# Both norms' roots in one GpSimd pair, row normalisation on GpSimd, routing weights on VectorE

## The chip, the core and the metric

The kernel runs on one core of a Trainium2 chip. A core has five engines that run their own instruction lists side by side and wait for one another through semaphores: TensorE (PE in the profile; its loads of weights are PEld), VectorE (DVE), ScalarE (ACT), GpSimd (POOL), and SyncE (SP), which here only issues transfers. GpSimd also issues the transfers that scatter rows by a list of indices. The metric is the time of one execution on the device, in microseconds; less is better.

## What is computed

One layer of cross-attention and one mixture-of-experts layer over 64 x 64 = 4096 tokens of 256 numbers each:

```
q = rms(linear(layernorm(x)))          k = rms(linear(ctx))        v = linear(ctx)
x = x + linear(softmax(q k' / 4) v)    # 16 heads of 16, 64 keys for each of 64 batches
h = layernorm(x)
two experts of 8 for each token by the largest logits of h, weights from their softmax
x = x + sum over the two: weight * W2 (silu(Wg h) * (Wu h))    # inner width 176
```

Both layernorms are (x - mean) / sqrt(variance + 1e-5), without scale and shift. For two experts with logits a >= b the weights are 1 / (1 + e) and e / (1 + e), with e = exp(b - a).

## The kernel before, in words

The tokens stand in 32 tiles of 128. A first stage, attention and routing, is a software pipeline over these tiles, written out in full: in turn i each engine works on several tiles at several depths. `Tile(j, s)` is tile n = 4j + s, `slot` its place in rings of four (s mod 4), `par` in pairs of buffers; `tile(3)` in turn i is tile i - 3, `tile(-2)` is tile i + 2. Each engine's `turn` function fixes the order of its work, and no scheduler changes it. Turns 0 to 34 have work for all engines, GpSimd's go on to turn 38. A second stage runs the experts: rows of tokens sorted by expert come back from memory in 71 slots of 128 rows, go through TensorE, and are scattered to their results by GpSimd (`send_y`); TensorE sets the pace of that stage, and the change touches nothing in it.

In a turn i of the first stage, as far as the change goes:

- TensorE transposes k of tile i - 1 (`tr_k`, the first work of its turn), then x of tile i, finds the largest scores of tile i - 2, weighs the values of tile i - 3, transposes q of tile i - 1 (`tr_q`), projects k, v and q of tile i, in even turns counts rows per expert for a pair of tiles (`count_rows`), scores tile i - 2, and last projects the attention of tile i - 3 (`project_out`).
- VectorE takes remainders of ScalarE's casts (`k_lo`, `xt_lo`, `q_lo`, `att_lo`: numbers go to TensorE as a high and a low part), the maxima, `normalise`, the statistics of the first norm of tile i + 2 (`ln1_stats`, `ln1_mean`), `ln2_norm` (the second norm applied to tile i - 4: a row of 256, subtract the mean, multiply by the root), then `att_lo`, then in odd turns `choose` (the two best experts of a pair of tiles), in even turns `route` (their places among the sorted rows), then `gate_of_x`, `k_scale`, `q_scale` with the roots from `qk_rms`, and last `residual` (x plus attention, the logits, the statistics and `ln2_mean` of tile i - 3). In turns 21 to 24 and 29 it also writes parts of the plan for the expert stage.
- GpSimd has `ctx_lo` (a remainder), `send(t, 1)` and `send(t, 0)` (the scatter of a tile's rows to its second and first expert, L545), `qk_rms` (the roots that scale q and k of tile i: two columns), `ln1` (root and shift of the first norm of tile i + 2), `weights` in even turns (the pair's two expert weights), `set_ids`, `ln2` (root of the second norm of tile i - 3), and `weights_lo` (a remainder of the expert weights). A root is two instructions: multiply and add (L499), then raise to the power -0.5 (L501).
- ScalarE applies the first norm to tile i + 1 (`ln1_norm`), casts, squares, takes exponentials, copies a normalised row (`row_copy`) and takes e for the pair (`gap_exp`).
- SyncE loads x in five parts, the last two in its turns 3 and 5 (L404), and spreads q and v over SBUF; the later parts of x are waited for once each, at tiles 2, 8 and 9, by `ln1_stats`.

The waits are `need` or `wait_ge` on counts of tiles done, and a waiting instruction holds all that stands behind it on its engine.

Of the kernel before, what the change touches and what calls it, by code (L numbers as in the profile page):

```python
# [93 lines left out]
def build_in(nc, stack, x, ctx_t, w_proj, w_out, w_exp, w_gate, bias, norm_q, norm_k, out,  # L94
# [378 lines left out]
    def _(pool):  # L473
# [44 lines left out]
        def ln2(t):  # L518
            need_alone(pool, pool_passed, S["row_ready"], t.n - 1)
            inv_sqrt(t, rstd2[:, t.slot, :], veps2[:, t.par, :], mean_var2[:, t.par, 1:2], 1.0, 1e-5,  # L520
                     S["ln2_mean"], S["ln2_veps"], S["ln2_rstd"])

        def weights(a, b, pp):

            need_alone(pool, pool_passed, R["e_gap_ready"], (a.pair + 1) * 2)
            need_alone(pool, pool_passed, S["row2_ready"], b.n + 1)
            w = row[:, :, a.slot:a.slot + 2, D + 1:D + 2].rearrange("p k m d -> p k (m d)")
            pool.tensor_scalar(one_e[:, :], e_gap[:, pp, :], 1.0, 1.0, ALU.mult, ALU.add).then_inc(R["weight_set1"], 1)
            need_alone(pool, pool_passed, R["weight_set1"], a.pair + 1)
            pool.tensor_tensor(w[:, 0, :], one_e[:, :], one_neg[:, :], ALU.pow).then_inc(R["weight_set2"], 1)  # L530
            need_alone(pool, pool_passed, R["weight_set2"], a.pair + 1)
            pool.tensor_tensor(w[:, 1, :], e_gap[:, pp, :], w[:, 0, :], ALU.mult).then_inc(R["weight_set3"], 1)
# [1205 lines left out]
```

## Time and profile before

| | us |
|---|---|
| three runs | 491.95, 491.39, 489.05 (median 491.39) |
| span of the profiled execution, first to last instruction | 489.1 |
| TensorE busy | 438.3 |
| VectorE busy | 391.4 |
| GpSimd busy | 308.6 |
| ScalarE busy | 276.7 |

The page gives no time of the profiled execution besides its span. The first stage lasts to about 309 us, the expert stage to about 475, and the rest adds up results. A busy share is an average over a whole stretch; what sets the pace is read from the order in time, from what an engine was waiting for when it stood still, and from the distance between the same instruction in one turn and in the next.

### The profile page before, as it was taken

The page shows a single profiled execution, that of the slowest core. Times are in us where ns is not written, and L with a number is a line of the kernel's source. Part 1 is how long each engine was busy: PE and PEld are TensorE (multiplying, and loading weights), DVE is VectorE, ACT ScalarE, POOL GpSimd, SP SyncE. Part 2 cuts the span into 40 slices and gives each one's busy share as a digit, 9 for nine tenths or more (in the row PEclk, how much of TensorE's full clock was granted, in tenths as well). Part 3 has the DMA queues.
Part 4 walks back from the last instruction along what each step waited for, and adds up shares of the span by engine and source line. Part 5 has one row for each costly group of instructions (what it writes and reads, how often), then busy time and mean ns, then how long its engine had stood idle before and what let it go on. Part 6 is the DMA issues. An engine that isn't in the chain of part 4 may idle for free.

```text
span 489.1 us, 15233 instructions
## 1 busy us (share of the span) xinstructions
PE 438.3 (90%) x4428; PEld 381.4 (78%) x4428; DVE 391.4 (80%) x1327; ACT 276.7 (57%) x802; POOL 308.6 (63%) x529
## 2 busy tenths in 40 slices
PE   7898999999999999898999888798999999999960
PEld 3568888888888788787888777587899999888850
DVE  7547788888888888889899787679876767898964
ACT  5355666666666566566666653454566656555630
POOL 6843458878788787876878865764344444454550
PEclk9999999999999999999999999999999999999995
DMA  6252453323323333223343324545344445879727
GB/s 207 78 161 73 137 165 88 117 86 92 104 86 112 89 91 104 81 89 100 89 118 86 88 83 105 160 155 150 99 131 121 131 125 167 271 244 294 255 98 258
DMA packets 55514, 64.62 MB, mean 132 GB/s; under 512 B 9599, under 2 KB 49034, under 8 KB 55434
## 3 DMA queue, kind: packets, MB, share of 16 engines
q1 hardware_dynamic: 44602, 42.59, 31.2%
q0 software_dynamic: 6480, 16.85, 9.7%
q10 hardware_dynamic: 4352, 4.20, 2.5%
q8 instruction: 39, 0.64, 0.6%
q14 instruction: 41, 0.34, 0.2%
HBM read 32.73 MB, written 23.14 MB: 114 GB/s over the span
## 4 chain that ended last, share of the span: by engine, by line
PE 41%; POOL 27%; issue 15%; DVE 13%; DMA 2%; ACT 1%; POOLq 1%; DVEq 0%; ACTq 0%; SPq 0%
POOL sorted_rows L545 8%; PE bank L1368 8%; PE bank L1369 7%; PE bank L1370 7%; PE bank L1609 4%; POOL r_qk L501 3%; POOL we_l L493 3%; POOL ct_l L487 2%; POOL rstd L501 2%; POOL row L530 2%; PE bank L1641 1%; PE bank L1642 1%; PE bank L1429 1%; PE bank L1631 1%; PE bank L1630 1%
## 5 line engine op out<-in xcount | busy, mean ns | idle before, releaser
L617 POOL DMA_INDIRECT expert_out<-probs,late x71 | 72.5, 1021 | 78.9 <-ACT probs L803 74.5
L545 POOL DMA_INDIRECT sorted_rows<-row,place_i x64 | 69.1, 1080 | 33.4 <-POOL row L537 15.6
L1368 PE MATMUL bank<-we_h,xt_h 128*128 x142 | 52.0, 366 | 2.5 <-DVE xt_l L1278 2.3
L708 ACT ACTIVATE probs<-bank 128x1024 f32<-128x1024 f32 x32 | 32.8, 1026 | 23.4 <-PE bank L1482 21.5
L791 ACT ACTIVATE xn<-bank 128x176 f32<-128x176 f32 x71 | 22.6, 318 | 41.4 <-PE bank L1370 41.4
L1369 PE MATMUL bank<-we_l,xt_h 128*128 x142 | 45.9, 324 | 0.0
L1370 PE MATMUL bank<-we_h,xt_l 128*128 x142 | 45.8, 322 | 0.0
L1288 DVE SCALAR_TENSOR_TENSOR probs<-xn,late,bank 128x128 f32<-128x128 f32 x71 | 24.4, 344 | 20.6 <-ACT xn L791 20.4
L501 POOL TENSOR_TENSOR rstd<-veps,half_neg 128x1 f32<-128x1 f32 x64 | 36.7, 573 | 5.3
L935 DVE TENSOR_REDUCE bank<-bank 128x16 f32<-128x1024 f32 x32 | 39.1, 1223 | 1.1 <-PE bank L1417 1.1
L803 ACT COPY probs<-bank 128x256 f32<-128x256 f32 x71 | 26.5, 373 | 18.9 <-PE bank L1642 16.7
L1278 DVE TENSOR_TENSOR xt_l<-bank,xt_h 128x256 fp32r<-128x256 f32 x71 | 30.1, 423 | 6.8 <-ACT xt_h L785 3.9
L1482 PE MATMUL bank<-neg_max_t,head_of 128*128 128x128 bf16 x256 | 35.2, 219 | 0.0
L1478 PE MATMUL bank<-qp,late 128*128 128x256 f16 x128 | 34.9, 273 | 0.0
L1479 PE MATMUL bank<-qp,late 128*128 128x256 f16 x128 | 34.9, 273 | 0.0
L1480 PE MATMUL bank<-qp,late 128*128 128x256 f16 x128 | 34.9, 273 | 0.0
L1429 PE MATMUL bank<-v_bd,probs 128*64 128x34 f32 x1024 | 34.7, 222 | 0.2 <-ACT probs L708 0.2
L1609 PE MATMUL bank<-ident,late 128*128 128x128 f32 x142 | 29.5, 289 | 5.6 <-issue 4.6
L673 ACT COPY neg_max_t<-bank 128x128 bf16<-128x128 bf16 x32 | 8.5, 265 | 43.4 <-PE bank L1458 43.4
L1429 PEld LDWEIGHTS bank<-v_bd,probs 128*64 128x64 f32 x1024 | 32.7, 138 | 0.4 <-ACT probs L708 0.4
L785 ACT CAST xt_h<-bank 128x256 fp32r<-128x256 f32 x71 | 26.6, 375 | 9.2 <-PE bank L1609 7.3
L1376 PE MATMUL bank<-bias_hl,ones_row 128*128 128x264 f32 (+1 forms) x96 | 30.8, 321 | 0.0
(237 smaller groups left out, 1596.4 us busy)
## 6 DMA issues: line engine op xcount, KB each, us to landing
late<-sorted_rows SPq DMA_DIRECT2D x71, 129.0 KB, 2.2
we_f<-w_exp SPq DMA_DIRECT2D x32, 152.0 KB, 2.6
v_bd<-v_sb SPq DMA_DIRECT2D x128, 34.0 KB
ctx_in<-ctx_t SPq DMA_DIRECT2D x32, 128.0 KB, 2.7
qp<-q_hl SPq DMA_DIRECT2D x128, 32.0 KB
x<-x SPq DMA_DIRECT2D x3, 1024.0 KB, 5.9
row<-expert_out SPq DMA_DIRECT2D x6, 512.0 KB, 5.1
qp<-expert_out SPq DMA_DIRECT2D x4, 512.0 KB, 4.3
```

Source lines behind the costliest of these rows:

```text
L501: pool.tensor_tensor(out_, tmp, half_neg[:, 0:tmp.shape[1]], ALU.pow).then_inc(done_, 1)
L545: pool.indirect_dma_start(sorted_rows, bass.IndirectOffsetOnAxis(ap=place_i[:, t.slot // 2, k, t.par:t.par + 1], axis=0), row[:, k, t.slot ...
L617: pool.indirect_dma_start(expert_out, bass.IndirectOffsetOnAxis(ap=hs(r)[:, D:D + 1].bitcast(U32), axis=0), y_sb[:, r % YRING, :], None, b ...
L935: dve.tensor_reduce(row_max, score_bank.rearrange("p (h k) -> p h k", h=NH), AX.X, ALU.max).then_inc(S["max_found"], 1)
L1368: pe.matmul(dst, a_h, b_h, start=start, stop=False)
L1369: pe.matmul(dst, a_h, b_l, start=False, stop=False)
L1370: return pe.matmul(dst, a_l, b_h, start=False, stop=stop)
L1429: ins = pe.matmul(av_bank[b * L:(b + 1) * L, g * 2 * VW:(g + 1) * 2 * VW], probs[:, t.par, at:at + L], v_bd[:, t.par, b, :, g * VW:(g + 1) ...
L1478: pe.matmul(dst, k_h, q_h, start=True, stop=False)
L1479: pe.matmul(dst, k_h, q_l, start=False, stop=False)
L1482: ins = pe.matmul(dst[:, gh * P:(gh + 1) * P], head_of[:, (b * KC + c) * NQ // 2 + gh, :], neg_max_t[:, t.par, :], start=False, stop=gh == ...
L1609: ins = pe.transpose(bank[:, p, c * P:(c + 1) * P], hs(r)[:, c * P:(c + 1) * P], ident[:, :])
```

## The change

Four things change place. `ln_roots` takes the root of the first norm of tile i + 2 and that of the second norm of tile i - 4 in one pair of GpSimd instructions, as two columns, at the start of GpSimd's turn; `ln1` and `ln2` are gone. `row_norm` on GpSimd takes over what `ln2_norm` did on VectorE. `weights` moves from GpSimd to VectorE, where it stands behind `route`, and takes a reciprocal in place of the power -1. On VectorE `choose`, `route` and `weights` now stand ahead of `att_lo`, `k_scale` ahead of `gate_of_x`, and the statistics of the first norm are those of tile i + 3, not i + 2.

```diff
+RSTDS = 8
+        self.ln1 = (self.n - 2) % RSTDS
+        self.ln2 = (self.n + 4) % RSTDS
...
-    mean_var = sb("mean_var", [P, 2, 2], F32)
-    veps = sb("veps", [P, SKEW, 1], F32)
-    rstd = sb("rstd", [P, SKEW, 1], F32)
+    mean_var = sb("mean_var", [P, 2, 2, 2], F32)
+    veps = sb("veps", [P, RSTDS, 2], F32)
+    rstd = sb("rstd", [P, RSTDS, 2], F32)
...
+        def ln_roots(one, two):
+            cols = slice(0 if one.live else 1, 2 if two.live else 1)
+            par, ring, done_ = one.par, one.ln1, one.n + 1
+            if one.live:
+                pool.wait_ge(S["ln1_mean"], one.n + 1)
+            if two.live:
+                pool.wait_ge(S["ln2_mean"], two.n + 1)
+            pool.tensor_scalar(veps[:, ring, cols], mean_var[:, par, cols, 1], 1.0, 1e-5, ALU.mult, ALU.add
+                               ).then_inc(S["ln_veps"], 1)
+            pool.wait_ge(S["ln_veps"], done_)
+            pool.tensor_tensor(rstd[:, ring, cols], veps[:, ring, cols], half_neg[:, cols], ALU.pow
+                               ).then_inc(S["ln_rstd"], 1)
+            pool.wait_ge(S["ln_rstd"], done_)
+            if one.live:
+                need(pool, S["xn_ready"], one.n - 1)
+                pool.tensor_scalar(shift[:, par, :], mean_var[:, par, 0, 0:1], rstd[:, ring, 0:1], -1.0,
+                                   ALU.mult, ALU.mult).then_inc(S["ln1_shift"], 1)
+
+        def row_norm(t):
+            if t.n >= SKEW:
+                pool.wait_ge(row_sent[0][t.slot], t.quad * 16)
+            pool.wait_ge(S["ln_rstd"], t.n + 7)
+            pool.tensor_scalar(row[:, 0, t.slot, 0:D], x1[:, t.n, :], mean_var[:, t.par, 1, 0:1], rstd[:, t.ln2, 1:2],
+                               ALU.subtract, ALU.mult).then_inc(S["row_ready"], 1)
...
         def turn(j, s):
+            if Tile(j, s + 2).live or Tile(j, s - 4).live:
+                ln_roots(Tile(j, s + 2), Tile(j, s - 4))
             if Tile(j, s + 1).live:
                 ctx_lo(Tile(j, s + 1))
             if Tile(j, s - 7).live:
                 send(Tile(j, s - 7), 1)
+            if Tile(j, s - 4).live:
+                row_norm(Tile(j, s - 4))
             if Tile(j, s).live:
                 qk_rms(Tile(j, s))
-            if Tile(j, s + 2).live:
-                ln1(Tile(j, s + 2))
-            if s % 2 == 0 and Tile(j, s - 6).live:
-                weights(Tile(j, s - 6), Tile(j, s - 5), (s - 6) // 2 % 2)
             if Tile(j, s - 6).live:
                 set_ids(Tile(j, s - 6))
                 send(Tile(j, s - 6), 0)
-            if Tile(j, s - 3).live:
-                ln2(Tile(j, s - 3))
             if Tile(j, s).live:
                 weights_lo(Tile(j, s))
...
+        def weights(a, b, pp):
+            dve.wait_ge(R["e_gap_ready"], (a.pair + 1) * 2)
+            w = row[:, :, a.slot:a.slot + 2, D + 1:D + 2].rearrange("p k m d -> p k (m d)")
+            dve.tensor_scalar(one_e[:, :], e_gap[:, pp, :], 1.0, None, ALU.add).then_inc(R["weight_set1"], 1)
+            dve.wait_ge(R["weight_set1"], a.pair + 1)
+            dve.reciprocal(w[:, 0, :], one_e[:, :]).then_inc(R["weight_set2"], 1)
+            dve.wait_ge(R["weight_set2"], a.pair + 1)
+            dve.tensor_tensor(w[:, 1, :], e_gap[:, pp, :], w[:, 0, :], ALU.mult).then_inc(R["weight_set3"], 1)
...
-            ahead = tile(-2) if tile(-2).live else None
+            ahead = tile(-3) if tile(-3).live else None
...
+            if isinstance(j, int) and j == s == 0:
+                ln1_stats(tile(-2), x_second)
+                ln1_mean(tile(-2))
             if ahead:
-                n = j * SKEW + s + 2 if isinstance(j, int) else None
-                ln1_stats(ahead, {2: x_second, 8: x_third, 9: x_rest}.get(n))
+                ln1_stats(ahead, {8: x_third, 9: x_rest}.get(ahead.n))
                 ln1_mean(ahead)
-            if tile(4).live:
-                ln2_norm(tile(4))
-            if tile(3).live:
-                att_lo(tile(3))
             if s % 2 == 1 and tile(5).live:
...
                 choose(a, tile(4), (s - 5) // 2 % 2)
             if s % 2 == 0 and tile(6).live:
                 route(tile(6), tile(5), (s - 6) // 2 % 2)
+                weights(tile(6), tile(5), (s - 6) // 2 % 2)
+            if tile(3).live:
+                att_lo(tile(3))
             if isinstance(j, int) and j == s == 0:
                 fold_gate()
             if tile(0).live:
+                k_scale(tile(0))
                 gate_of_x(tile(0))
-                k_scale(tile(0))
                 q_scale(tile(0))
```

GpSimd's list, one odd turn and the start of the even one behind it in the middle of the first stage, of the kernel before; a row is line, operation, output<-inputs and size.

```order
L487 TENSOR_TENSOR ct_l<-ctx_in,ct_h 128x256
L545 DMA sorted_rows<-row,place_i 33920x258
L499 TENSOR_SCALAR ms_eps<-sumsq 128x2
L501 TENSOR_TENSOR r_qk<-ms_eps,half_neg 128x2
L499 TENSOR_SCALAR veps<-mean_var 128x1
L501 TENSOR_TENSOR rstd<-veps,half_neg 128x1
L508 TENSOR_SCALAR shift<-mean_var,rstd 128x1
L537 COPY row<-result_row 128x2
L545 DMA sorted_rows<-row,place_i 33920x258
L499 TENSOR_SCALAR veps<-mean_var 128x1
L501 TENSOR_TENSOR rstd<-veps,half_neg 128x1
L493 TENSOR_TENSOR we_l<-we_f,we_h 128x304
```

The same turn of the changed kernel, on GpSimd (`rstd` and `veps` are now of both norms, `row<-x` is `row_norm`).

```order
L510 TENSOR_SCALAR veps<-mean_var 128x2
L513 TENSOR_TENSOR rstd<-veps,half_neg 128x2
L518 TENSOR_SCALAR shift<-mean_var,rstd 128x1
L486 TENSOR_TENSOR ct_l<-ctx_in,ct_h 128x256
L547 DMA sorted_rows<-row,place_i 33920x258
L525 TENSOR_SCALAR row<-x,mean_var,rstd 128x256
L498 TENSOR_SCALAR ms_eps<-sumsq 128x2
L500 TENSOR_TENSOR r_qk<-ms_eps,half_neg 128x2
L539 COPY row<-result_row 128x2
L547 DMA sorted_rows<-row,place_i 33920x258
L492 TENSOR_TENSOR we_l<-we_f,we_h 128x304
```

The roots of the norms moved to the front of the turn, in one pair of two columns; `row_norm` stands between the first dispatch and `qk_rms` (`ms_eps`, `r_qk`).

VectorE's list in turn 6, of the kernel before, with the semaphores that each instruction waits for (`x_third` and `x_rest` are loads of x).

```order
L959 TENSOR_TENSOR att<-bank,r_sum 128x256 [waits att_transposed,sum_inverted]
L910 BN_STATS stats<-x 128x6 [waits x_third]
L915 BN_AGGR mean_var<-stats 128x2 [waits ln1_stats,xn_ready]
L1003 TENSOR_SCALAR row<-x,mean_var,rstd 128x256 [waits ln2_rstd]
L966 TENSOR_TENSOR at_l<-bank,at_h 128x256 [waits o_projected,at_h_ready]
L1032 TENSOR_TENSOR place<-bank,filled 128x16 [waits routed]
L1036 TENSOR_TENSOR filled<-filled,bank 128x8 [waits place_ready]
L1038 TENSOR_TENSOR place_of<-chosen,place 128x32
L1042 TENSOR_REDUCE place_f<-place_of 128x4 [waits place_sel]
L1048 CAST place_i<-place_f 128x4 [waits place_sum]
L985 TENSOR_SCALAR x_gate<-bank,veps,rstd 128x8 [waits q_squared]
L975 TENSOR_SCALAR late<-bank,r_qk 128x2x8x16 [waits k_transposed,v_ready,qk_rstd]
```

The same turn of the changed kernel, on VectorE.

```order
L909 BN_STATS stats<-x 128x6 [waits x_rest]
L914 BN_AGGR mean_var<-stats 128x2 [waits ln1_stats,ln1_shift]
L1024 TENSOR_TENSOR place<-bank,filled 128x16 [waits routed]
L1028 TENSOR_TENSOR filled<-filled,bank 128x8 [waits place_ready]
L1030 TENSOR_TENSOR place_of<-chosen,place 128x32
L1034 TENSOR_REDUCE place_f<-place_of 128x4 [waits place_sel]
L1040 CAST place_i<-place_f 128x4 [waits place_sum]
L1046 TENSOR_SCALAR one_e<-e_gap 128x2 [waits e_gap_ready]
L1048 RECIPROCAL row<-one_e 128x2 [waits weight_set1]
L1050 TENSOR_TENSOR row<-e_gap,row 128x2 [waits weight_set2]
L965 TENSOR_TENSOR at_l<-bank,at_h 128x256 [waits o_projected,at_h_ready]
L974 TENSOR_SCALAR late<-bank,r_qk 128x2x8x16 [waits k_transposed,v_ready,qk_rstd]
```

`at_l` (`att_lo`) moved behind `route` and `weights`, the row of 256 is gone, and the statistics of this turn wait for another load.

GpSimd's list at the start of turn 0, of the kernel before.

```order
L610 MEMSET qp 128x2048
L487 TENSOR_TENSOR ct_l<-ctx_in,ct_h 128x256
L499 TENSOR_SCALAR ms_eps<-sumsq 128x2
L501 TENSOR_TENSOR r_qk<-ms_eps,half_neg 128x2
L499 TENSOR_SCALAR veps<-mean_var 128x1
L501 TENSOR_TENSOR rstd<-veps,half_neg 128x1
L508 TENSOR_SCALAR shift<-mean_var,rstd 128x1
```

The same of the changed kernel, on GpSimd.

```order
L609 MEMSET qp 128x2048
L510 TENSOR_SCALAR veps<-mean_var 128x1
L513 TENSOR_TENSOR rstd<-veps,half_neg 128x1
L518 TENSOR_SCALAR shift<-mean_var,rstd 128x1
L486 TENSOR_TENSOR ct_l<-ctx_in,ct_h 128x256
L498 TENSOR_SCALAR ms_eps<-sumsq 128x2
L500 TENSOR_TENSOR r_qk<-ms_eps,half_neg 128x2
```

The three instructions for tile 2's first norm moved ahead of `ctx_lo` and of the roots for q and k of tile 0.

## Rows read from the trace of the kernel before

**Rows 1.** Busy time by stretch: PE, PEld, DVE, ACT, POOL; PEclk, DMA, GB/s.

```profile
150.00:185.00 35.00, 32.91 (x415) 28.90 (x416) 30.31 (x109) 22.22 (x65) 28.31 (x54) 1.00 0.34 95
```

**Rows 2.** GpSimd in time order: start, us, line, operation, tiles, [idle before <-releaser].

```profile
150.78 1.09 POOL L545 DMA_INDIRECT sorted_rows<-row,place_i  x1 [0.81 <-DVE mean_var L997]
...
160.15 1.09 POOL L545 DMA_INDIRECT sorted_rows<-row,place_i  x1 [0.81 <-POOL row L537]
...
168.23 1.09 POOL L545 DMA_INDIRECT sorted_rows<-row,place_i  x1 [0.81 <-DVE mean_var L997]
```

**Rows 3.** TensorE in time order: first tr_k of turns, count_rows, project_out.

```profile
20.44 0.66 PE L1394 MATMUL bank<-ident,late 128*128 128x128 f32 x4 [0.72 <-DVE late L975]
...
70.32 0.60 PE L1394 MATMUL bank<-ident,late 128*128 128x128 f32 x4
...
149.14 0.66 PE L1394 MATMUL bank<-ident,late 128*128 128x128 f32 x4 [1.07 <-DVE late L975]
...
154.44 0.17 PE L1526 MATMUL bank<-chosen_b,ones_b 128*128 128x8 bf16 x1
...
156.44 0.37 PE L1368 MATMUL bank<-wp_h,at_h 128*128 128x264 f32 x1
...
157.38 0.60 PE L1394 MATMUL bank<-ident,late 128*128 128x128 f32 x4
...
166.60 0.66 PE L1394 MATMUL bank<-ident,late 128*128 128x128 f32 x4 [1.06 <-DVE late L975]
...
290.13 0.66 PE L1394 MATMUL bank<-ident,late 128*128 128x128 f32 x4 [0.25 <-DVE late L975]
```

**Rows 4.** VectorE in time order: turn 6's statistics, then one even turn.

```profile
66.58 0.42 DVE L910 BATCH_NORM_STATS2 stats<-x 128x6 f32<-128x256 f32 x1
...
150.37 0.18 DVE L997 BATCH_NORM_AGGREGATE mean_var<-stats 128x2 f32<-128x6 f32 x1
...
154.25 0.42 DVE L1003 TENSOR_SCALAR row<-x,mean_var,rstd 128x256 f32<-128x256 f32 x1
155.32 0.42 DVE L966 TENSOR_TENSOR at_l<-bank,at_h 128x256 fp32r<-128x256 f32 x1 [0.65 <-ACT at_h L702]
155.66 0.16 DVE L1032 TENSOR_TENSOR place<-bank,filled 128x16 f32<-128x16 f32 x1
...
156.46 0.28 DVE L985 TENSOR_SCALAR x_gate<-bank,veps,rstd 128x8 f32<-128x8 f32 x1
...
166.06 0.48 DVE L975 TENSOR_SCALAR late<-bank,r_qk 128x256 f32<-128x256 f32 x1 [0.70 <-POOL r_qk L501]
```

**Rows 5.** GpSimd's groups by line and form: count | busy us, mean ns | idle.

```profile
L501 POOL TENSOR_TENSOR rstd<-veps,half_neg 128x1 f32<-128x1 f32 x64 | 36.7, 573 | 5.3
...
L487 POOL TENSOR_TENSOR ct_l<-ctx_in,ct_h 128x256 fp32r<-128x256 f32 x32 | 24.0, 749 | 3.8 <-ACT ct_h L656 3.8
L501 POOL TENSOR_TENSOR r_qk<-ms_eps,half_neg 128x2 f32<-128x2 f32 x32 | 23.4, 732 | 2.8 <-POOL ms_eps L499 0.2
L499 POOL TENSOR_SCALAR veps<-mean_var 128x1 f32<-128x1 f32 x64 | 12.0, 188 | 14.7 <-DVE mean_var L997 7.0 <-DVE mean_var L915 3.0
...
L508 POOL TENSOR_SCALAR shift<-mean_var,rstd 128x1 f32<-128x1 f32 x32 | 8.5, 267 | 3.3
```

**Rows 6.** ScalarE in time order: end of q_square in the same even turn.

```profile
154.79 0.19 ACT L686 ACTIVATION_READ_ACCUMULATOR square<-bank 128x1 f32 x1
```

**Rows 7.** Line 404, the last loads of x: issues, then time to landing.

```profile
L404 SPq DMA_DIRECT2D x<-x x2: 583/585/587, 47.0 to 65.1; - x2
...
DMA to landing us min/median/max: 5.6/5.8/5.9
```

**Rows 8.** TensorE by stretch, after its last matmul: us, busy, PEclk, DMA, GB/s.

```profile
474.00:475.00 1.00, 0.00 (x0) 0.86 0.03 8
```

**Rows 9.** VectorE and GpSimd in time order, at the start.

```profile
7.99 1.22 DVE L891 TENSOR_TENSOR wp_l<-probs,wp_h 128x1024 fp32r<-128x1024 f32 x1
8.18 1.45 POOL L501 TENSOR_TENSOR rstd<-veps,half_neg 128x1 f32<-128x1 f32 x1
```

More of the change, by code:

```diff
@@ L329, in build_in @@
     block = stack.enter_context(nc.Block())
-    SETUP_POOL = 21
-    SETUP_POOL_FIRST = 6
+    SETUP_POOL = 20
+    SETUP_POOL_FIRST = 5
     SETUP_DVE = 15
@@ L516, in qk_rms @@
                      S["k_squared"], S["qk_veps"], S["qk_rstd"])
[L518 to L532, printed above, removed]
         def set_ids(t):
@@ L586, in _ @@
                                  base=0, pattern=[[1, NE], [-1, NE]], channel_multiplier=0))
-        ln1(Tile(0, 0))
-        ln1(Tile(0, 1))
+        ln_roots(Tile(0, 0), Tile(0, -6))
+        ln_roots(Tile(0, 1), Tile(0, -5))
         ctx_lo(Tile(0, 0))
@@ L637, in ln1_norm @@
             act.activation(xn[:, t.par, :], x1[:, t.at, :], ACT.Identity, bias=shift[:, t.par, :],
-                           scale=rstd[:, t.slot, :]).then_inc(S["xn_ready"], 1)
+                           scale=rstd[:, t.ln1, 0:1]).then_inc(S["xn_ready"], 1)
         def k_hi(t):
@@ L711, in gap_exp @@
             act.wait_ge(R["gap_ready"], a.pair + 1)
-            act.wait_ge(S["ln2_rstd"], b.n + 1)
+            act.wait_ge(S["ln_rstd"], b.n + 7)
             for m, t in enumerate((a, b)):
-                act.activation(e_gap[:, pp, m:m + 1], gap[:, pp, m:m + 1], ACT.Exp, scale=rstd2[:, t.slot, :]
+                act.activation(e_gap[:, pp, m:m + 1], gap[:, pp, m:m + 1], ACT.Exp, scale=rstd[:, t.ln2, 1:2]
                                ).then_inc(R["e_gap_ready"], 1)
@@ L912, in ln1_mean @@
         def ln1_mean(t):
-            need(dve, S["xn_ready"], t.n - 1)
+            need(dve, S["ln1_shift"], t.n - 1)
             need_alone(dve, dve_passed, S["ln1_stats"], t.n + 1)
-            dve.bn_aggr(mean_var[:, t.par, :], stats[:, t.par, :]).then_inc(S["ln1_mean"], 1)
+            dve.bn_aggr(mean_var[:, t.par, 0, :], stats[:, t.par, :]).then_inc(S["ln1_mean"], 1)
         def xt_lo(t):
@@ L984, in gate_of_x @@
             dve.wait_ge(S["q_squared"], t.n + 1)
-            dve.tensor_scalar(x_gate[:, t.slot, :], qp_bank[:, gate_cols], veps[:, t.slot, :], rstd[:, t.slot, :],
+            dve.tensor_scalar(x_gate[:, t.slot, :], qp_bank[:, gate_cols], veps[:, t.ln1, 0:1], rstd[:, t.ln1, 0:1],
                               ALU.mult, ALU.mult).then_inc(S["x_gate_ready"], 1)
@@ L996, in residual @@
             need_alone(dve, dve_passed, S["ln2_stats"], t.n + 1)
-            dve.bn_aggr(mean_var2[:, t.par, :], stats2[:, t.par, :]).then_inc(S["ln2_mean"], 1)
-        def ln2_norm(t):
-            dve.wait_ge(S["ln2_rstd"], t.n + 1)
-            if t.quads_ok:
-                dve.wait_ge(row_sent[0][t.slot], t.quad * 16)
-            dve.tensor_scalar(row[:, 0, t.slot, 0:D], x1[:, t.at, :], mean_var2[:, t.par, 0:1], rstd2[:, t.slot, :],
-                              ALU.subtract, ALU.mult).then_inc(S["row_ready"], 1)
+            dve.bn_aggr(mean_var[:, t.par, 1, :], stats2[:, t.par, :]).then_inc(S["ln2_mean"], 1)
         def choose(a, b, pp):
@@ L1205, in rows_last @@
         def rows_last():
-            a, b = last_tiles()
-            ln2_norm(b)
             dve.wait_ge(S["weighed"], NT)
@@ L1213, in route_last @@
             route(a, b, a.pair % 2)
+            weights(a, b, a.pair % 2)
             dve.wait_ge(R["filled_new"], NT // 2)
```

18 lines of the change are left out of this document (3 added, 15 removed).

## The prediction

> **What bounds the kernel now.** I first read the table of busy time by stretch [rows 1], to see whether one engine fills the attention stage. In 35 us from its middle TensorE is busy 32.91 and GpSimd 28.31, so neither is the bound by its busy share. The order in time decides. On GpSimd I took the gap from one dispatch of a first row (`send(t, 0)`) to the next [rows 2]: 150.78, 160.15, 168.23, so 9.37 us for the even turn, which holds `weights`, and 8.08 us for the odd one. Between these rows GpSimd waits for no other engine: what is not busy is the 0.81 us ahead of each of these dispatches, which has the same length in even and odd turns whatever releaser is named, and the 0.1 to 0.2 us between instructions. So its order alone needs 17.45 us a pair.
>
> TensorE's turn, from its first `tr_k` matmul to the next [rows 3], takes 157.38 - 149.14 = 8.24 us and 166.60 - 157.38 = 9.22 us, together 17.46: the same. It has one stall in the pair, 1.06 us at 166.60, for `k_scale` on VectorE; and `k_scale` had waited 0.70 us for `r_qk`, GpSimd's work [rows 4]. **So in this stretch GpSimd is the bound, through `r_qk`**, and TensorE alone would need 8.24 and 9.22 - 1.06 = 8.16, about 8.2 us a turn. From turn 7 to turn 32 the mean is (290.13 - 70.32) / 25 = 8.79 us [rows 3].
>
> **What the change removes and adds on GpSimd, a turn.** Second norm's pair gone: 0.19 + 0.57 us [rows 5] and a gap, 0.81. First norm's root becomes two columns wide: the trace has a root of two columns at 0.73 against 0.57 for one [rows 5], so +0.16. `weights` is gone from even turns: 9.37 - 8.08 = 1.29. New: `row_norm`, x us, with a gap of 0.08. All turns become 8.08 - 0.81 + 0.16 + 0.08 + x = 7.51 + x.
>
> No row shows x, a one-input operation over 256 columns on GpSimd. From below: the same operation over one column takes 0.19 us. From above: a subtraction of 256 columns with two inputs takes 0.75 us [rows 5]; `shift`, which reads a scalar, takes 0.08 more than `veps`, which doesn't, so 0.83. One input has half of the two-input operation's reading: I take 0.55, just above the middle. Then GpSimd needs 8.06 us a turn (7.70 to 8.34), under TensorE's 8.2: it stops being the bound, narrowly.
>
> The Trainium skill speaks against this move: "GPSIMD Engine Reference", section 8, calls VectorE about twice as fast for elementwise work, and its section 4.1 limits that to two-input operations, with one-input ones roughly at line rate. By the first sentence x would be about twice `ln2_norm`'s 0.42 us on VectorE [rows 4], an estimate of 0.84; by the second it stays near what I took. The page's two-input rule fits the trace (0.75 us for 256 columns [rows 5]). The first reading is rival B.
>
> **What it adds and moves on VectorE.** `ln2_norm` (0.42 us [rows 4]) goes; `weights` comes into even turns as three dependent operations on two columns, each 0.2 from start to start as the steps of `route` are [rows 4], but 0.1 after the last: 0.5. More important is the order. `choose`, `route` and `weights` now stand ahead of `att_lo`. `att_lo` starts at 155.32 after an idle 0.65, and `route` takes 155.66 to 156.46, 0.80 us [rows 4]. `route` needs the counts, whose last matmul ends at 154.44 + 0.17 = 154.61; so `route` would run from 154.67, `weights` to 155.97, `att_lo` to 156.39, and TensorE's `project_out` starts at 156.44 [rows 3, 4]. It just fits; I set 0.06 us a turn for misses, with ends 0 and 0.25. `x_gate` behind `k_scale` instead of ahead of it costs nothing while `q_scale` is ready before `tr_q`, two microseconds into TensorE's next turn.
>
> `qk_rms` now stands behind `ln_roots`, `send(t, 1)` and `row_norm`, where before only `ctx_lo` and the send were ahead. It has to wait for ScalarE's `q_square` anyway, which ends at 154.79 + 0.19 = 154.98, 5.84 us into TensorE's turn [rows 6, 3]. The roots can start with the second norm's mean, 150.37 + 0.18 = 150.55, 1.41 us in [rows 4]; 1.35 for them, 0.75 for `ctx_lo`, 0.17 and 1.09 for the dispatch and 0.63 for `row_norm` end at 5.40. The cover is 0.4 us; where it is gone, each missing tenth is a tenth a turn.
>
> Gain: 25 turns at 8.2 need 205.0 of today's 219.8 us, so 14.8 at most. Off that: four turns (22 to 25), in which VectorE also writes the early plan, keep 0.7 us each by my estimate (2.8), as that work stays; and 0.06 on the other 21 turns (1.3). **-10.7 us**, with ends -14.8 and, at x = 0.83 (0.09 more than 8.25 on 21 turns), -8.8.
>
> **What two moves cost at the start, once each.**
> First, in turn 0 `ln_roots` for tile 2 stands ahead of `ctx_lo(1)` and `qk_rms(0)`. Its mean is ready by then, so there is no wait, but its three operations run first: 0.19 + 0.57 + 0.27 with gaps, some 1.2 us. That is on the path: before its first `tr_k`, at 20.44, TensorE sits 0.72 idle for `k_scale` [rows 3], which waits for `r_qk`. **+1.2 us**.
>
> Second, VectorE's statistics of the first norm run a tile earlier (`tile(-3)`), and the wait on `x_rest`, which hangs on tile 9, moves from turn 7 to turn 6. SyncE issues the last part of x at 65.1, and it lands 5.6 to 5.9 us later, near 70.9 [rows 7]. Turn 6's statistics stand at 66.58 [rows 4]: VectorE would stop for 4.3 us, and behind it `route`, `weights` and `att_lo`, for which `project_out` waits. From 70.9: 0.62 for statistics and mean, 0.80 and 0.50 for `route` and `weights`, 0.42 for `att_lo`, 0.06 to signal, and `project_out` with 157.38 - 156.44 = 0.94: the next `tr_k` at 74.2 to 74.3 instead of 70.32 [rows 3]. **+4.0 us**. The load cannot come sooner: SyncE issues it behind the spreads of tile 4, which follow `q_lo(4)` in turn 5, as before. Ends: 0, if the load lands with no other traffic beside it and in time, and 4.6.
>
> A TensorE idle for 4 us may lose its clock: at the end of the kernel, from 474 to 475, no matmul runs and the mean granted clock is 0.86, so within that microsecond it falls to the lower of its levels, 1.2 GHz [rows 8]. The work after the stop would then run at half rate for some time. I put **+0.8 us**, ends 0 and 4 (as much again as the stop). "TensorE: Matmul & The Clock Gate" of the Trainium skill, section "Why this matters for your kernels", warns of idle gaps between bursts of matmuls; the trace agrees in so far as the clock falls after idling.
>
> The end: the last rows' dispatches lose one `weights` (1.29) and gain row_norm, and the first expert slots wait for `row_norm(31)` on GpSimd some 0.6 us longer; I set 0, ends -1 and +1.
>
> Sum: -10.7 + 1.2 + 4.0 + 0.8 = **-4.7 us**. The profiled execution has a span of 489.1 us; the page shows nothing around it, and it stands 2.3 below the median of 491.4. Span after: 484.4; median after: **486.7 us**.
>
> **The rivals.**
> A, the forecast: 486.7 (484 to 489 with its small terms). Chance 0.45.
> B, GpSimd stays the bound: `row_norm` takes 0.84 to 0.95. Against: one input only. For: the sum is within 0.3 us of TensorE's. At 0.84 the gain is -8.6, the time 488.8; at 0.95 (8.46 a turn) -6.3, the time 491.1. Chance 0.25.
> C, slower: `row_norm` is held up by VectorE. Each turn VectorE and GpSimd would touch SBUF together; at 8.18 a one-column root took 1.45 us instead of 0.57 while VectorE subtracted two SBUF operands [rows 9]. "SBUF — State Buffer" (section "SBUF: two separate sides") of the Trainium skill calls this an exclusive lock; the trace agrees. With 0.65 more than 0.55, x = 1.2, GpSimd needs 17.42 us a pair, nothing is gained in 21 turns but 0.05 each, and 6.0 is paid: about 496.5. It turns from gain to loss near x = 0.97, where GpSimd's turn is 8.48 and the gain 5.9. Against it: at `row_norm`'s place VectorE reads PSUM, or a single SBUF tile, or very small ones. Chance 0.09.
> D, the wait for x costs nothing visible: 486.7 - 4.8 = 481.9. For it: DMA queues at the start are uneven. Against: 4.3 us is missing. Chance 0.21.
>
> **How the numbers follow.** About 1% (4.9 us) can be told from no change. A lies across the border of 486.5, so half of it (0.22) and D (0.21) are faster: 0.43. C is slower: 0.09. The rest, 0.48, is within 1%. The range reaches from just below D to just above B: 481.5 to 492.
>
> **What would show it.** Right: `tr_k` to `tr_k` near 8.2 us in even and odd turns, no stall on `k_scale`; a row of `row_norm` near 0.55 us; the first `tr_k` 1.2 us later; a single VectorE wait for the load of x of some 4 us in turn 6. Wrong: GpSimd still without a wait in mid-stage and `row_norm` over 0.8 us (B or C); no VectorE wait for x (D); regular stalls of `project_out` on `at_l`, which would mean that the new order on VectorE doesn't fit.

## The result, and the profile after

The changed kernel is slower: 502.8 us (median of four runs, 500.0 to 504.5) against 491.5 for the kernel before, a ratio of 1.023 with a 95% interval of 1.019 to 1.027. The forecast was 486.7 us, with 481.5 to 492.0 as its range. The span of the profiled execution is 498.3 us instead of 489.1. The ratios below are to runs of the kernel before that stand beside each experiment (medians 490.7 to 491.7). Medians and ratios leave out runs over 1.5% above the fastest of their kernel: two of twelve with `row_norm` back on VectorE, and one of six with the start mended.

First the turns. These are rows of TensorE's `tr_k` (the first work of its turn) of the kernel after, in order of time: start, us, line, operation, tiles, [idle before <-releaser]; they answer to [rows 3].

```profile
21.62 0.66 PE L1396 MATMUL bank<-ident,late 128*128 128x128 f32 x4 [2.00 <-DVE late L974]
...
75.72 0.60 PE L1396 MATMUL bank<-ident,late 128*128 128x128 f32 x4
84.03 0.60 PE L1396 MATMUL bank<-ident,late 128*128 128x128 f32 x4
...
162.83 0.66 PE L1396 MATMUL bank<-ident,late 128*128 128x128 f32 x4 [0.31 <-DVE late L974]
171.57 0.66 PE L1396 MATMUL bank<-ident,late 128*128 128x128 f32 x4 [0.38 <-DVE late L974]
...
296.35 0.60 PE L1396 MATMUL bank<-ident,late 128*128 128x128 f32 x4
```

Set beside the same rows of before, the difference grows in five places and stands still between them:

| first `tr_k` of turn | before | after | difference |
|---|---|---|---|
| 1 | 20.44 | 21.62 | +1.2 |
| 2 | 27.62 | 29.85 | +2.2 |
| 6 | 62.09 | 63.98 | +1.9 |
| 8 | 79.55 | 84.03 | +4.5 |
| 22 | 201.79 | 206.57 | +4.8 |
| 26 | 238.40 | 244.41 | +6.0 |
| 32 | 290.13 | 296.35 | +6.2 |
| first silu of the expert stage (ScalarE) | 313.94 | 323.35 | +9.4 |
| span | 489.1 | 498.3 | +9.2 |

So the 14 turns from 8 to 22, where most of the gain of 10.7 us was to come from, take 8.75 us each instead of 8.73: nothing gained. What is lost comes from the start (turns 1 and 2), the stop for x between turns 6 and 8, the turns with the plan (22 to 26), and the passage to the experts.

GpSimd in order of time, one turn of after from one first dispatch (`send(t, 0)`) to the next; it answers to [rows 2].

```profile
154.38 1.11 POOL L547 DMA_INDIRECT sorted_rows<-row,place_i  x1 [0.81 <-POOL row L539]
155.52 0.84 POOL L492 TENSOR_TENSOR we_l<-we_f,we_h 128x304 fp32r<-128x304 f32 x1
156.45 0.19 POOL L510 TENSOR_SCALAR veps<-mean_var 128x2 f32<-128x2 f32 x1
156.73 0.72 POOL L513 TENSOR_TENSOR rstd<-veps,half_neg 128x2 f32<-128x2 f32 x1
157.55 0.26 POOL L518 TENSOR_SCALAR shift<-mean_var,rstd 128x1 f32<-128x1 f32 x1
157.78 0.73 POOL L486 TENSOR_TENSOR ct_l<-ctx_in,ct_h 128x256 fp32r<-128x256 f32 x1
158.76 1.08 POOL L547 DMA_INDIRECT sorted_rows<-row,place_i  x1 [0.25 <-issue]
159.91 1.27 POOL L525 TENSOR_SCALAR row<-x,mean_var,rstd 128x256 f32<-128x256 f32 x1
161.26 0.19 POOL L498 TENSOR_SCALAR ms_eps<-sumsq 128x2 f32<-128x2 f32 x1
161.54 0.72 POOL L500 TENSOR_TENSOR r_qk<-ms_eps,half_neg 128x2 f32<-128x2 f32 x1
...
163.22 1.11 POOL L547 DMA_INDIRECT sorted_rows<-row,place_i  x1 [0.81 <-POOL row L539]
```

8.84 us, with no wait for another engine: GpSimd is still the bound. `row_norm` (L525) takes 1.27 us here. The page's groups give its mean over all 32 tiles, and who waits for GpSimd:

```profile
L525 POOL TENSOR_SCALAR row<-x,mean_var,rstd 128x256 f32<-128x256 f32 x32 | 39.8, 1242 | 1.9
...
L974 DVE TENSOR_SCALAR late<-bank,r_qk 128x256 f32<-128x256 f32 x32 | 15.5, 484 | 27.3 <-POOL r_qk L500 27.3
```

1242 ns, where the forecast took 550; and `k_scale` (L974) waits 27.3 us in all for the roots that stand behind `row_norm`.

VectorE's statistics in turn 6, the stop for x (compare 66.58 in [rows 4]):

```profile
72.39 0.43 DVE L909 BATCH_NORM_STATS2 stats<-x 128x6 f32<-128x256 f32 x1 [3.69 <-DMA x<-x]
```

And the passage to the experts, GpSimd, ScalarE, VectorE and TensorE in order of time:

```profile
320.37 1.23 POOL L525 TENSOR_SCALAR row<-x,mean_var,rstd 128x256 f32<-128x256 f32 x1
...
321.63 0.41 ACT L667 COPY row<-row 128x256 f32<-128x256 f32 x1 [2.62 <-POOL row L525]
322.05 1.28 ACT L790 ACT_TABLE_LOAD   x1
...
323.35 0.32 ACT L790 ACTIVATE xn<-bank 128x176 f32<-128x176 f32 x1
...
323.69 0.35 DVE L1290 SCALAR_TENSOR_TENSOR probs<-xn,late,bank 128x128 f32<-128x128 f32 x1 [5.18 <-ACT xn L790]
...
324.32 0.47 PE L1632 MATMUL bank<-ident,probs 128*128 128x128 f32 x1 [3.94 <-DVE probs L1293]
```

The first silu (L790) stands on ScalarE behind the copy of the last row, and that behind `row_norm(31)`, on a GpSimd that waits for no other engine from 311.5 on. TensorE stands still for 3.94 us. This first row also tells something else: VectorE does nothing from 318.5 to 323.7, and `row_norm` takes 1.23 us all the same.

### The profile page after: what moved, and what is told of

It reads as the page before. It is cut to its first block, busy times and chain, and to the rows that moved or that the text cites. A ratio compares the mean times of both kernels' runs of the same rounds, so it can differ in the third digit from the quotient of the medians.

```text
span 498.3 us, 15165 instructions
## 1 busy us (share of the span) xinstructions
PE 443.0 (89%) x4428; PEld 385.2 (77%) x4428; DVE 388.0 (78%) x1343; ACT 276.3 (55%) x802; POOL 316.6 (64%) x460
## 4 chain that ended last, share of the span: by engine, by line
PE 42%; POOL 24%; issue 18%; DVE 10%; DMA 2%; ACT 1%; SPq 1%; POOLq 1%; DVEq 0%; ACTq 0%
POOL sorted_rows L547 9%; PE bank L1370 8%; PE bank L1371 8%; PE bank L1372 8%; PE bank L1611 4%; POOL rstd L513 4%; POOL r_qk L500 3%; POOL ct_l L486 2%; PE bank L1643 2%; PE bank L1644 2%; POOL row L525 1%; PE bank L1633 1%; PE bank L1632 1%; DMA x<-x 1%; POOL veps L510 1%
## 5 line engine op out<-in xcount | busy, mean ns | idle before, releaser
L790 ACT ACTIVATE xn<-bank 128x176 f32<-128x176 f32 x71 | 22.6, 318 | 42.4 <-PE bank L1372 42.4
L525 POOL TENSOR_SCALAR row<-x,mean_var,rstd 128x256 f32<-128x256 f32 x32 | 39.8, 1242 | 1.9
L974 DVE TENSOR_SCALAR late<-bank,r_qk 128x256 f32<-128x256 f32 x32 | 15.5, 484 | 27.3 <-POOL r_qk L500 27.3
L1370 PEld LDWEIGHTS bank<-we_h,xt_h 128*128 128x128 f32 x142 | 27.0, 190 | 5.2 <-issue 5.0
```

The lines of the kernel that those rows point to most:

```text
L525: pool.tensor_scalar(row[:, 0, t.slot, 0:D], x1[:, t.n, :], mean_var[:, t.par, 1, 0:1], rstd[:, t.ln2, 1:2], ALU.subtract, ALU.mult).then_ ...
L1370: pe.matmul(dst, a_h, b_h, start=start, stop=False)
```

## The experiments

Theory 1: `row_norm` has a price of its own, 1.24 us, which puts back what the roots and `weights` took off GpSimd. Rival (the prediction's C): it costs about 0.55 and is held up by VectorE. A further rival: GpSimd isn't what paces the turns at all.

### The price of the operation by itself

```diff
...
+        def probe(ins):
+            n[0] += 1
+            ins.then_inc(probed, 1)
+            pool.wait_ge(probed, n[0])
+
+        h = half_neg[:, 0:1]
...
+        for quiet in (1, 0):
+            for _ in range(2):
+                probe(pool.tensor_scalar(po[:, 0:256], pi[:, 0:256], h, h, ALU.subtract, ALU.mult))
+                probe(pool.tensor_scalar(po[:, 0:128], pi[:, 0:128], h, h, ALU.subtract, ALU.mult))
+                probe(pool.tensor_scalar(po[:, 0:512], pi[:, 0:512], h, h, ALU.subtract, ALU.mult))
+                probe(pool.tensor_scalar(po[:, 0:256], pi[:, 0:256], h, None, ALU.mult))
+                probe(pool.tensor_scalar(po[:, 0:256], pi[:, 0:256], 0.5, 2.0, ALU.subtract, ALU.mult))
+                probe(pool.tensor_scalar(po[:, 0:256], pi[:, 0:256], 0.5, None, ALU.mult))
+                probe(pool.tensor_tensor(po[:, 0:256], pi[:, 0:256], pi[:, 256:512], ALU.subtract))
+                probe(pool.tensor_copy(po[:, 0:256], pi[:, 0:256]))
...
```

> The changed kernel and, after its results, GpSimd operations by themselves on dead parts of x: first with all other engines at rest, then with VectorE subtracting two SBUF operands of 512 columns without a pause. The result's rows are stored before. Theory 1 (a price of the operation itself): the two-operation form with two per-partition scalars over 256 columns takes 1.24 us at rest as well, about half of the part above 0.19 us at 128 columns (0.7 us), twice it at 512 (2.3 us); one operation, or immediate scalars, tell which of the two makes it dear (one operation near 0.75 if the price is per operation; immediates near 0.55 if it is the scalars). Theory 2 (VectorE holds the port, as in rival C of the prediction): 0.55 us at rest, 1.2 and more beside VectorE.

All of it stands behind the last sums, and each instruction waits for the one before it; for the second value of `quiet` VectorE subtracts 128x512 SBUF operands meanwhile. It is one execution, with each form twice in either condition. GpSimd in order of time; the lines 637 to 644 are the eight calls of the diff. First with all engines at rest, then, from 514.42 on, beside VectorE.

```profile
496.67 1.22 POOL L637 TENSOR_SCALAR x<-x,half_neg 128x256 f32<-128x256 f32 x1 [10.67 <-DVEq L1385]
497.99 0.80 POOL L638 TENSOR_SCALAR x<-x,half_neg 128x128 f32<-128x128 f32 x1
498.88 2.07 POOL L639 TENSOR_SCALAR x<-x,half_neg 128x512 f32<-128x512 f32 x1
501.06 0.93 POOL L640 TENSOR_SCALAR x<-x,half_neg 128x256 f32<-128x256 f32 x1
502.08 1.08 POOL L641 TENSOR_SCALAR x<-x 128x256 f32<-128x256 f32 x1
503.24 0.86 POOL L642 TENSOR_SCALAR x<-x 128x256 f32<-128x256 f32 x1
504.19 0.72 POOL L643 TENSOR_TENSOR x<-x 128x256 f32<-128x256 f32 x1
504.98 0.40 POOL L644 COPY x<-x 128x256 f32<-128x256 f32 x1
...
514.42 1.66 POOL L637 TENSOR_SCALAR x<-x,half_neg 128x256 f32<-128x256 f32 x1 [0.22 <-POOL x L644]
...
524.07 0.72 POOL L643 TENSOR_TENSOR x<-x 128x256 f32<-128x256 f32 x1
```

Theory 1 holds: 1.22 us at rest, 1.23 the second time. From 256 to 512 columns it grows by 0.85, so 3.3 ns a column and some 0.4 fixed. The second operation is worth 0.22 to 0.29 us (1.08 - 0.86, 1.22 - 0.93), scalars from memory 0.07 to 0.14; but even the simplest `tensor_scalar` with one operation and a constant (0.86) is dearer than a subtraction of two tensors (0.72), and only the bare copy is cheap (0.40). A busy VectorE adds 0.31 to 0.44 (1.54 and 1.66): the hold-up of rival C exists, but in the kernel `row_norm` takes 1.22 to 1.28 us over its 32 tiles, next to none of it.

### `row_norm` back on VectorE, and split in two

Back on VectorE (all else as changed):

```diff
@@ gpsimd @@
-            if Tile(j, s - 4).live:
-                row_norm(Tile(j, s - 4))
...
@@ vector @@
                 ln1_mean(ahead)
+            if tile(4).live:
+                row_norm(tile(4))
...
```

> The changed kernel, with the row normalisation back on VectorE at its old place (behind the first norm's statistics), and all else as changed. Theory: row_norm's 1.24 us on GpSimd are what kept GpSimd the bound (8.75 us a turn); without them GpSimd needs 7.4 us a turn and TensorE's 8.2 to 8.3 set the pace: 24 turns x 0.45 to 0.55 = 11 to 13 us, and some 2 to 3 us at the passage to the experts, where row_norm(31) was waited for: 487 to 490. Rival 1: VectorE, which gets 0.42 us back and keeps weights (some 7.75 us busy a turn), becomes the bound near 8.5 us a turn: 495 to 497. Rival 2: GpSimd is not what paces the turns: no change, 502 to 503.

Split, columns 0 to 127 on GpSimd and 128 to 255 on VectorE:

```diff
@@ gpsimd @@
-            pool.tensor_scalar(row[:, 0, t.slot, 0:D], x1[:, t.n, :], mean_var[:, t.par, 1, 0:1], rstd[:, t.ln2, 1:2],
+            pool.tensor_scalar(row[:, 0, t.slot, 0:P], x1[:, t.n, 0:P], mean_var[:, t.par, 1, 0:1], rstd[:, t.ln2, 1:2],
...
@@ vector @@
+            dve.tensor_scalar(row[:, 0, t.slot, P:D], x1[:, t.n, P:D], mean_var[:, t.par, 1, 0:1], rstd[:, t.ln2, 1:2],
...
```

> The changed kernel, with row_norm split: columns 0 to 127 stay on GpSimd, columns 128 to 255 go to VectorE. The probe gave 0.80 us for 128 columns on GpSimd where 256 take 1.22. Theory (GpSimd's turn is 7.51 + x): 8.31 us a turn instead of 8.75, still a little over TensorE's 8.2, so a turn of 8.3 to 8.35; with the stop for x left in, and 3 x 0.4 us less in the passage, about 491 (24 x 0.44 + 1.2 = 11.8 less than 502.8). Rival: GpSimd's turn isn't the bound that x adds to (a fixed wait elsewhere): turns stay at 8.75, 502.

The turns follow the price x of `row_norm` on GpSimd (mean of turns 8 to 22):

| | x, us | 7.51 + x | measured turn | time, ratio to before |
|---|---|---|---|---|
| changed | 1.24 | 8.75 | 8.75 | 502.8, 1.023 (1.019 to 1.027) |
| split | 0.80 | 8.31 | 8.34 | 495.7, 1.009 (1.006 to 1.011) |
| on VectorE | 0 | 7.43 (its gap of 0.08 goes too) | 8.24 | 489.3, 0.997 (0.994 to 1.000) |

So the prediction's formula 7.51 + x is right where GpSimd paces the turns, and TensorE's floor of 8.2 with it; only x was wrong. In the split kernel `k_scale` still waits 0.24 us a turn for GpSimd's roots; with `row_norm` on VectorE GpSimd itself waits, some 0.8 us a turn, for ScalarE's `q_square`. The turns did as told, but of the whole times only one lies in its forecast: with `row_norm` on VectorE 489.3 us (487 to 490), split 495.7 where about 491 was expected. What the turns gained was lost around them. The statistics waited longer for x (4.76 us with `row_norm` on VectorE, 4.56 split), and TensorE's clock fell around that stop; the split one's first `tr_k` came only at 22.42; and its passage to the experts, from `tr_k` of turn 32 to the first silu, took 27.8 us instead of the 27.0 of after, where 1.2 less was expected. One stretch (us, busy of PE, PEld, DVE, ACT, POOL, then PEclk, DMA, GB/s), first of after, then with `row_norm` on VectorE:

```profile
72.00:74.00 2.00, 0.00 (x0) 0.00 (x0) 1.37 (x9) 0.91 (x2) 0.00 (x0) 1.00 0.59 172
```

```profile
72.00:74.00 2.00, 1.47 (x7) 1.50 (x7) 1.40 (x5) 0.00 (x0) 0.85 (x1) 0.50 0.01 4
```

0.50 is the 1.2 GHz level. In after the clock stayed at 2.4 GHz over a stop of TensorE of 3.2 us and the turn from 7 to 8 took 8.31 us; with 4.6 us of idle it fell, and that turn took 9.32.

### The stop for x

```diff
-                ln1_stats(ahead, {8: x_third, 9: x_rest}.get(ahead.n))
+                ln1_stats(ahead, {8: x_third, 16: x_rest}.get(ahead.n))
```

> The changed kernel, with the wait for the last part of x hung on tile 16 (the first tile that lies in it) instead of tile 9. Theory: the 3.7 us stop of VectorE in turn 6 is the whole of the step from +1.9 to +5.4 us against the kernel before that the first tr_k of turn 7 shows; without it tr_k of turn 7 comes near 72.2 instead of 75.72, and as the changed kernel made up 0.9 us of the stop by turn 8, the gain at the end is 2.9 us: about 499.9 where the changed kernel took 502.8. Rival: GpSimd, which paces the turns, was behind anyway, and the stop cost nothing beyond turn 9: 502 to 503.

496.2 us, ratio 1.013 (1.009 to 1.016): better than expected by 3.7. The profile agrees with the theory where it can be compared: from turn 6 to turn 22 it takes 139.5 us instead of 142.6, so the stop is worth 3.1. The rest lies ahead of turn 6 (61.74 against 63.98), in a start that this edit doesn't touch and that differs between executions.

### The start

```diff
-            if Tile(j, s + 2).live or Tile(j, s - 4).live:
+            if (j or s) and (Tile(j, s + 2).live or Tile(j, s - 4).live):
                 ln_roots(Tile(j, s + 2), Tile(j, s - 4))
...
                 qk_rms(Tile(j, s))
+            if j == s == 0:
+                ln_roots(Tile(0, 2), Tile(0, -4))
```

> The changed kernel, with ln_roots behind qk_rms in turn 0 only, as in the kernel before. Theory: the first tr_k comes at 20.4 instead of 21.62 (1.2 us), and because TensorE then stands idle for less than a microsecond there, its granted clock does not fall at 22 to 26 us, which cost 1.05 us more by the second tr_k (29.85 against 27.62): 2.2 us less, about 500.6. Rival: the clock falls for another reason than this wait; then only 1.2 us are gained, 501.6.

500.7 us, ratio 1.020 (1.016 to 1.024), whose interval overlaps that of the changed kernel: the time doesn't decide. Nor does this profile by itself. Its first `tr_k` comes at 20.56 and its second at 27.77, with no fall of the clock; but GpSimd's setup ended at 16.8 us here and at 18.0 in after, and in two profiles where it ended as early with the start left as changed, these rows stand at 20.34 and 27.52 (`row_norm` on VectorE) and at 20.61 and 27.82 (the probe). What the order is worth shows where the setup ends late, under "Why the prediction was wrong".

By turn 22 only 0.7 us were left. This profile was 3.0 us ahead of after at turn 6, 1.6 at turn 7 and 0.4 at turn 8. SyncE issued the last part of x sooner too (63.92 instead of 66.53), and the statistics that need it started 2.4 us sooner; but VectorE waited 4.32 us for it instead of 3.69, and TensorE's clock fell during the stop (0.68 at 70 to 72 us, 0.50 from 72 to 76), which it hadn't done in after. Why it fell here and not there isn't shown.

### The passage to the experts

```diff
+            late = j * SKEW + s > NT
+            if late and Tile(j, s - 4).live:
+                row_norm(Tile(j, s - 4))
             if Tile(j, s - 7).live:
                 send(Tile(j, s - 7), 1)
-            if Tile(j, s - 4).live:
+            if not late and Tile(j, s - 4).live:
                 row_norm(Tile(j, s - 4))
```

> The changed kernel, with row_norm ahead of the second rows' dispatch from turn 33 on. Theory: the experts' first silu on ScalarE stands behind the copy of the last row, which waits for row_norm(31) on GpSimd (ends 321.6; ScalarE waited 2.6 us, TensorE 3.9 us and then ran at half clock); one dispatch (1.06 us and its 0.8 us gap) less ahead of it brings the first silu 1.9 us sooner: 500 to 501. Rival: what the first expert slots wait for is the transfer of rows or the plan, not row_norm(31): 502 to 503.

500.4 us, ratio 1.020 (1.016 to 1.024), an interval that again overlaps that of the changed kernel. In the profile the gain is where it was looked for: from `tr_k` of turn 32 to the first silu it takes 24.8 us, where after took 27.0 and before 23.8: 2.2 of the 3.2 us lost there (1.9 were expected).

All three at once, `row_norm` still on GpSimd in every turn:

> The changed kernel with its three side costs mended at once (wait for x on tile 16, ln_roots behind qk_rms in turn 0, row_norm ahead of the second dispatch from turn 33 on) and row_norm still on GpSimd. Theory: the turns themselves (8.75 us against 8.73 before) neither gain nor lose, and all that the change lost lies in these three places: 1.9 + 2.6 + 2.2 of the 9.4 us, so 494 to 496, still some 2 to 4 us over the kernel before (turns 22 to 26 took 1.2 us longer, the passage 1.0 more). Rival: something else in the changed kernel costs: 498 and more.

496.8 us, ratio 1.010 (1.008 to 1.013): above the 494 to 496 expected, and no better than the stop mended alone. The turns are at 8.74, so nothing else is hidden there. But its turn from 7 to 8 took 12.0 us: with the stop for x gone, TensorE stood still for 2.43 us ahead of its scores, and its clock fell.

```profile
72.73 0.64 PE L1424 MATMUL bank<-late,qp 128*64 128x128 f16 x16 [2.43 <-issue]
```

The profile names no releaser; of what this matmul waits for, only the spread of q can have been under way still. SyncE had issued it at 65.96, 0.7 behind the last part of x (1.3 to 2.4 us behind it in the profiles of the other kernels without the stop). The clock fell once more in the passage, after turn 32 (0.50 at 300 to 302 us). Whether the order of those two transfers is what delays the spread was not tried. The three gains don't add up, and this run doesn't show whether that is the rule or chance.

### `weights` alone, and VectorE's new order

The kernel before, with only `weights` moved to VectorE, behind `route`, and with the change's reciprocal:

```diff
@@ gpsimd @@
-            if s % 2 == 0 and Tile(j, s - 6).live:
-                weights(Tile(j, s - 6), Tile(j, s - 5), (s - 6) // 2 % 2)
...
@@ vector @@
                 route(tile(6), tile(5), (s - 6) // 2 % 2)
+                weights(tile(6), tile(5), (s - 6) // 2 % 2)
...
```

> The kernel before, with only weights moved to VectorE (behind route); the norms' roots and the row normalisation stay as they were. Theory: GpSimd's even turns lose 1.29 us and come to 8.08, so that TensorE's 8.2 us a turn set the pace: the mean of turns 7 to 32 falls from 8.79 to 8.2 to 8.35, 11 to 14 us less than before: 478 to 481. Rival 1: weights' 0.5 us on VectorE, behind att_lo, come ahead of k_scale in even turns and eat the gain: 486 to 490. Rival 2: GpSimd's order was not the bound in the kernel before: 490 to 492.

489.5 us, ratio 0.997 (0.995 to 1.000): the 486 to 490 of rival 1, and hardly a gain. The turn fell from 8.73 to 8.49 only. VectorE in order of time, around its only idle time in a turn:

```profile
168.16 0.63 DVE L990 TENSOR_SCALAR row<-x,mean_var,rstd 128x256 f32<-128x256 f32 x1
169.22 0.42 DVE L953 TENSOR_TENSOR at_l<-bank,at_h 128x256 fp32r<-128x256 f32 x1 [0.43 <-ACT at_h L689]
169.56 0.16 DVE L1019 TENSOR_TENSOR place<-bank,filled 128x16 f32<-128x16 f32 x1
```

GpSimd now waits 0.5 us a turn for ScalarE's `q_square`: it isn't the bound. VectorE is, with 8.05 us from wait to wait and 0.43 of waiting for `at_h`, while `route` (L1019), which then runs without a wait, stands behind `att_lo`. (In turns 8 to 22 `ln2_norm`, L990, takes 0.60 us here and 0.41 in the next kernel; why isn't shown.) The next kernel adds to it the change's own order on VectorE:

```diff
-            if tile(3).live:
-                att_lo(tile(3))
             if s % 2 == 1 and tile(5).live:
                 ...
                 weights(tile(6), tile(5), (s - 6) // 2 % 2)
+            if tile(3).live:
+                att_lo(tile(3))
...
-                gate_of_x(tile(0))
                 k_scale(tile(0))
+                gate_of_x(tile(0))
```

> The kernel of e4_weights (the kernel before, weights on VectorE), with VectorE's new order of the change: choose, route and weights ahead of att_lo, k_scale ahead of gate_of_x. No merged roots, no row_norm, the first norm's statistics as before. Theory: in e4 VectorE had become the bound, at 8.49 us a turn, of which it waits 0.44 us for at_h ahead of att_lo while route or choose stand behind it; with these ahead the wait is filled, VectorE needs 8.05 us and TensorE's 8.15 to 8.2 set the pace: 24 turns x 0.3 = 7 us less than e4's 489.5, 481 to 483.5. Rival: att_lo then comes late for project_out and TensorE waits there instead: 487 to 490.

483.0 us, ratio 0.984 (0.982 to 0.986), a turn of 8.18. TensorE fills its time. Turns 8 to 22 of before and of this kernel (us, busy of PE, PEld, DVE, ACT, POOL, then PEclk, DMA, GB/s):

```profile
79.50:201.80 122.30, 114.89 (x1436) 100.94 (x1436) 105.70 (x379) 78.33 (x227) 98.86 (x190) 1.00 0.34 97
```

```profile
77.80:192.30 114.50, 114.48 (x1437) 101.51 (x1436) 106.22 (x400) 76.85 (x225) 90.48 (x169) 1.00 0.36 103
```

Nearly the same TensorE work, 114.9 and 114.5 us, in 122.3 and in 114.5 us.

Last, the changed kernel with the edits on `row_norm` (VectorE), x and start together:

> The kernel of e3_norm_dve (row normalisation on VectorE), with the wait for the last part of x on tile 16 and ln_roots behind qk_rms in turn 0. Theory: e3 ran its turns at 8.15 us from turn 8 to 22, but lost its gain to the stop for x: from turn 6 to turn 8 it took 23.2 us where two turns take 16.4. Without the stop that gives 6.8 us back: 482.5 to 484.5 where e3 took 490.1, clearly faster than the kernel before. Rival: the pace of 8.15 us is only the making up of the stop, or what follows (the dispatches, the plan, the passage to the experts) takes the gain: 487 to 490.

482.9 us, ratio 0.984 (0.981 to 0.986), a turn of 8.22 (the 8.15 expected was too low: with the stop left in it is 8.24), and no stop between turns 6 and 8 (16.7 us). So two versions beat the kernel before by the same 1.6%; the one without merged roots is the smaller edit.

## Why the prediction was wrong, point by point

- **What bounds the kernel: right.** GpSimd paced the kernel before, and TensorE alone needs 8.2. Between them VectorE showed itself at 8.49 when `weights` moved there without the new order, which is not what the change runs. The prediction asked of the new order only that it fit (0.06 us a turn). It does fit, and it is worth 0.3 us a turn once GpSimd is out of the way.
- **The cost of `row_norm`: the step that failed.** "One input has half of the two-input operation's reading: I take 0.55", between 0.19 and 0.83. It costs 1.24, above the upper end. The upper end was a `tensor_tensor` plus the price of reading a scalar, and that is no upper end for a `tensor_scalar` with two operations, by 0.4 us. With x = 1.24 the prediction's own formula gives 8.75 us a turn, as measured, and a gain of nothing instead of 10.7; with its three costs of 6.0 that is 497.4. The Trainium skill's "GPSIMD Engine Reference", section 4.1, calls one-input operations on GpSimd roughly line-rate; the copy's 0.40 us beside VectorE's 0.42 for `ln2_norm` [rows 4] agrees, the 0.86 to 1.22 of the four forms of `tensor_scalar` over 256 columns do not, and the measurement decides. The Trainium skill's blanket factor of two for elementwise work (section 8 of that page; rival B's 0.84) was too low as well. Rival B had the mechanism, GpSimd staying the bound, with too small a price; the signs that the prediction set for B or C, GpSimd without a wait and `row_norm` over 0.8 us, are what the trace shows.
- **Rival C: its x right by luck, its mechanism wrong.** Its x of 1.2 is nearly the measured one, and the time it gave (496.5) is the nearest of the four, but VectorE didn't hold `row_norm` up: it takes 1.23 us beside an idle VectorE and 1.22 at rest.
- **The start: size right where GpSimd's setup ends late.** +1.2 us, as worked out: of the five profiles in which that setup ended at 18.0 to 18.3 us, the three with the old order in turn 0 have the first `tr_k` at 20.4 to 20.6, the two with the new one at 21.6 and 21.9. Where the setup ended at 16.6 to 17.0 us, the new order gives 20.3 to 21.0, so the cost isn't paid in every execution (the split kernel's setup ended at 17.3, but GpSimd then waited 1.6 us for `q_square`: 22.4). Not foreseen: TensorE idled 2.0 us there, its clock fell at 22 to 26 us (0.55 and 0.60), and another 1.0 was lost by turn 2.
- **The stop for x: right in place and nearly in size.** 3.69 us instead of 4.3; 2.6 at turn 8, as some was made up (3.1 by its own experiment). Rival D, no visible wait, falls.
- **The clock behind that stop: +0.8 was about right, as a mean.** Of the six profiles with the stop it fell in all but after's, and there the turn behind cost 1.0 to 1.4 us more than the 8.31 of after.
- **Plan turns 22 to 26:** taken as 8.9 us each, they take 9.46 (9.35 even with `row_norm` on VectorE, and 9.15 before).
- **The end: set to 0, measured +3.2.** The prediction put in one `row_norm` (0.6). But GpSimd has no pause in the last turns, so `row_norm` counts in each of them, and `row_norm(31)` stands behind a dispatch too; ScalarE's first silu waits for it all. Taking one dispatch from ahead of it gave 2.2 of the 3.2 back. The other 1.0 stays open: with `row_norm` off GpSimd altogether the passage still takes 24.8 to 26.5 us, against 23.8 before.

The sum in terms of the profile: start 1.9, stop 2.6, turns 1.7, passage 3.2, experts -0.2, together +9.2 us of span. The medians lie 11.3 apart: the profiled execution is the fastest of the four, and where the others spend 1.5 to 4.5 us more isn't on record.

## What to carry to other kernels

Before an elementwise operation is moved to another engine, take its price there from the same instruction form at the same width, not from a neighbour with more inputs; where no row has it, a probe of eight instructions behind the end of the kernel settles it. When the engine that paces a loop is relieved, look for the next one a few tenths behind it, and for an instruction there that waits while ready work stands behind it: that reordering gave 6.5 of the 8 us that were to be had. Hang a wait for a transfer on its first real use: moved there, the wait for the last part of x gave back 3.1 us, and with the wait left where it was, most of a lead of 3.0 us was gone two turns behind it.
